# A recurrence with packed side work: one piece per step from the group's start, bare steps last, and gelus in halves

## The chip, the core and the metric
The kernel is one program on one core of a Trainium2 chip. The metric is the device time of one execution in microseconds (us), of which the median of three runs is shown. Five engines run side by side, each in its own order: TensorE (PE, with its weight loads as PEld), VectorE (DVE), ScalarE (ACT), GpSimd (POOL) and SyncE (SP). They meet only at semaphores.

## What is computed
The input x has 4 sequences of 1024 tokens with 128 features. The reference is a chain of six layers:

```python
x = x + 0.5 * _L0_ffn_ref(_layernorm(x), ...)      # small attention over 4 positions, then 8 experts, top 2
x = x + _L0_attn_ref(_layernorm(x), ...)           # hierarchical attention
x = x + 0.5 * _L0_ffn_ref(_layernorm(x), ...)      # the same expert layer again
x = x + 0.5 * _L1_ffn_ref(_layernorm(x), ...)      # sign weights, 128 -> 512 -> 128
x = x + _L1_attn_ref(_layernorm(x), ...)           # recurrence of 1024 steps, then an MLP 128 -> 512 -> 128
x = x + 0.5 * _L1_ffn_ref(_layernorm(x), ...)      # sign weights again
```

The recurrence inside `_L1_attn_ref` is the part that can't be spread out:

```python
def step(state, inp):                               # state is 4 x 32
    xb_t, xd_t = inp
    state = jnp.tanh(state @ A.T + xb_t)
    out = state @ C.T + xd_t
    return (state, out)
```

## The kernel before
The program has three phases: the first expert layer, the hierarchical attention, and `routed_ffn_and_recurrence`, which merges the last four layers. The change touches only the third phase.

**Groups and steps.** The 1024 tokens are cut into 8 groups (`GROUPS`) of 128 tokens. Once two groups have been prepared, the third phase enters a loop over groups 0 to 7, and `body(g)` runs the 128 recurrence steps of group g on two engines. On PE, a step waits for the last tanh and issues one product of 4 columns (L1369). On ACT, a step waits for that product and takes one tanh (L1514). PE and ACT hand the state to each other 1024 times, so this is a chain that nothing shortens.

**Pieces.** All other work of the last four layers is cut into pieces that PE issues behind a step's product, before the next step's. `slots(g)` gives each piece the number of the step (its slot) in which it stands. These are the kinds, by the names that the prediction uses:
- a *small piece*: `up_half` or `k_up_half`, 256 columns against one weight tile (L1170, L1231), or `down_tile` of an expert, two products of 128 columns (L1180)
- a *transpose piece*: four 128x128 transposes (L1105), as `p_turn1`, `p_turn2`, `p_turn3` and `k_turn_tiles`
- a *large piece*: `k_down_tile` (L1242), four products of 128 columns; `p_proj` (L1132) has as many
- a *whole run*: several `up_whole` or `k_up_whole` of 512 columns (L1157, L1223) in one slot
- a *mix piece*: half of `mix_tiles` (L1264, L1266), which reads the recurrence's states with a stride as weights; two per group
- `p_qkv` (384 columns, L1119), `p_router` (L1145) and `input_product` (L1253), the last of which starts the next group's sums
- a *bare step* has no piece at all.

**What a group holds.** In group g the *expert part* (`routed_order`) computes the expert layer of group g+2: a whole run of four with the first expert's down tiles, then for each of the other experts 4 up halves and 4 down tiles, with the attention pieces of groups g+3 and g+4 between them. The *dense part* (`dense_order`) holds three 128 -> 512 -> 128 layers of three groups: a (sign weights, group g+1), r (the MLP, group g-1) and z (the last sign weights, group g-2). The mix pieces hand the recurrence's output of group g-1 to DVE, which makes r's input of it. Groups 6 and 7 have no expert part left.

**What sets the order.** `slots` gives each piece an assumed cost from the table `NS` and spreads the pieces over all 128 steps in proportion to it, so bare steps lie between pieces everywhere. ACT's gelus are put into slots by `plan_of`, one step or two behind their up piece. DVE's order is written out in `routed(m, g)` and `dense(g)`: norms, expert sums (`add_expert`, L882), layer outputs and the attention's elementwise work. POOL computes reciprocal roots. After the loop PE does the mix of group 7, then z of group 6, r of group 7 and z of group 7, one after another (L1400 on).

## Time and profile before
| | us |
|---|---|
| median of 3 runs (2312.71 to 2322.3) | 2315.91 |
| the profiled execution | 2301.93 |
| its span | 2300.1 |
| first tanh of the loop to the last | 1137.31 to 2249.13 |
| PE busy (matmul) | 1856.1, 81% |
| ACT busy | 830.5, 36% |
| DVE busy | 1010.4, 44% |
| mean granted TensorE clock | 0.745 |

The page gives the busy time of each engine over the whole span. Matmuls are pipelined, so a busy PE is not one at its peak. Its second part cuts the span in 40 slices and has a row PEclk with the clock that TensorE was granted, in tenths of full speed. The loop of 1024 steps takes the second half of the span. The timeline view has the single instructions, and behind each the idle time of its engine before it and what ended that.

### The profile page before, as it was taken

How to read it: one execution, taken by the hardware profiler on the slowest of the kernel's cores; microseconds unless marked ns; L12 is line 12 of the kernel's file. 1: busy time of each engine (PE TensorE's matmuls, PEld its weight loads, DVE VectorE, ACT ScalarE, POOL GpSimd, SP SyncE). 2: the span in 40 equal slices, each digit the busy share in tenths (PEclk: the TensorE clock that was granted, in tenths of full speed). 3: DMA queues.
4: the chain of work that ended last, by engine and by line, in shares of the span. 5: the costliest groups of instructions: out<-in, count | busy, mean ns of one | idle time of the engine just before them, and what ended most of it. 6: DMA issues, size and time to landing. Idle time of an engine off the chain costs nothing.

```text
span 2300.1 us, 36406 instructions
## 1 busy us (share of the span) xinstructions
PE 1856.1 (81%) x13438; PEld 1328.0 (58%) x13438; DVE 1010.4 (44%) x3005; ACT 830.5 (36%) x2192; POOL 193.5 (8%) x314
## 2 busy tenths in 40 slices
PE   2889995848688596758788998999989999978776
PEld 1666674536474474726655655666666666645555
DVE  3666654866777767645522223223232221121102
ACT  1444443546556464413333223233242222322222
POOL 1212201000010000021101001010000000000000
PEclk8999996979789697859986558577595555765557
DMA  5000000000000000000000000000000000000000
GB/s 151 1 1 1 0 1 1 2 1 3 2 2 2 1 2 2 2 0 1 1 1 1 1 0 1 0 1 5 1 5 1 1 5 0 1 5 1 5 0 14
DMA packets 12015, 13.06 MB, mean 6 GB/s; under 512 B 1649, under 2 KB 10641, under 8 KB 11281
## 3 DMA queue, kind: packets, MB, share of 16 engines
q1 hardware_dynamic: 11840, 10.77, 1.8%
q8 instruction: 105, 1.72, 0.3%
q14 instruction: 70, 0.57, 0.1%
HBM read 8.67 MB, written 2.10 MB: 5 GB/s over the span
## 4 chain that ended last, share of the span: by engine, by line
issue 53%; POOL 3%; POOLq 2%; PE 0%; DVE 0%; ACT 0%; ACTq 0%; SPq 0%; DVEq 0%
POOL m_pairs L706 1%; POOLq L673 1%; POOL m_root_p L716 0%; POOL m_roots L697 0%; POOL m_root_r L716 0%; POOLq L715 0%; POOL m_root_a L716 0%; POOL m_root_z L716 0%; PE m_post_misc L1242 0%; PE m_down L1231 0%; PE m_up L1231 0%; POOLq L688 0%; POOL m_roots L690 0%; POOLq L686 0%; POOLq L684 0%
## 5 line engine op out<-in xcount | busy, mean ns | idle before, releaser
L1514 ACT ACTIVATE m_state<-m_scan 32x4 f32<-32x4 f32 x1024 | 166.3, 162 | 776.8 <-PE m_scan L1369 776.0
L1369 PEld LDWEIGHTS m_scan<-m_state,rnnA 128*32 128x32 f32 x2048 | 173.4, 131 | 375.3 <-issue 191.8
L1369 PE MATMUL m_scan<-m_state,rnnA 128*32 128x4 f32 x2048 | 262.0, 198 | 107.4 <-ACT m_state L1514 107.4
L882 DVE SCALAR_TENSOR_TENSOR x_all<-m_down,m_weight,x_all 128x128 f32<-128x128 f32 x256 | 71.9, 343 | 447.6 <-PE m_down L1180 447.6
L1180 PE MATMUL m_down<-moe,m_hT 128*128 128x128 f32 x1024 | 242.2, 390 | 4.8 <-ACT m_hT L1460 3.7
L1180 PEld LDWEIGHTS m_down<-moe,m_hT 128*128 128x128 f32 x1024 | 193.9, 272 | 14.0 <-ACT m_hT L1460 5.7
L1170 PE MATMUL m_up<-m_x2T,moe 128*128 128x256 f32 x384 | 189.8, 606 | 5.0 <-ACT m_hT L1460 5.0
L2157 DVE TENSOR_TENSOR att_big<-at_ring,att_big 128x512 f16<-128x512 f32 x192 | 123.9, 685 | 49.0 <-ACT att_big L1839 48.2
L286 PEld LDWEIGHTS f_down<-moe,f_hT 128*128 128x128 f32 x1024 | 125.6, 195 | 27.9 <-issue 26.5
L1839 ACT ACTIVATE att_big<-at_ring 128x512 f16<-128x512 f32 x192 | 111.4, 596 | 66.1 <-PE at_ring L1972 64.0
L277 PE MATMUL f_up<-f_x2T,moe 128*128 128x512 f32 x256 | 123.6, 608 | 5.8 <-ACT f_hT L193 5.8
L286 PE MATMUL f_down<-moe,f_hT 128*128 128x128 f32 x1024 | 127.3, 278 | 0.0
L463 DVE SCALAR_TENSOR_TENSOR x_all<-f_down,f_weight,x_all 128x128 f32 (+1 forms) x256 | 72.0, 344 | 82.8 <-PE f_down L286 82.7
L1972 PE MATMUL at_ring<-at_keys,att_Mhi 128*128 128x512 f16 x256 | 81.6, 402 | 30.8 <-DVE at_coarse_q L2144 18.9
L193 ACT ACTIVATE f_hT<-f_up 128x512 f32<-128x512 f32 x128 | 74.9, 597 | 69.4 <-PE f_up L277 68.6
L2264 DVE SCALAR_TENSOR_TENSOR att_big<-at_ring,att_big 128x512 f16<-128x512 f32 x128 | 80.8, 682 | 27.1 <-ACT att_big L1880 27.0
L1170 PEld LDWEIGHTS m_up<-m_x2T,moe 128*128 128x128 f32 x384 | 86.0, 271 | 11.0 <-ACT m_hT L1460 6.7
L2062 PE MATMUL at_s<-att_Nhi,att_big 128*128 128x128 f16 x1024 | 92.3, 221 | 0.0
L1880 ACT ACTIVATE att_big<-at_ring 128x512 f16<-128x512 f32 x128 | 68.7, 602 | 61.6 <-PE at_ring L2053 61.2
L2062 PE MATMUL at_s<-att_Nlo,att_big 128*128 128x128 f16 x512 | 88.9, 221 | 0.0
L1991 PE MATMUL at_s<-at_keys,att_big 128*128 128x16 f16 x768 | 72.1, 172 | 18.4 <-DVE att_big L2157 18.4
L1991 PEld LDWEIGHTS at_s<-at_keys,att_big 128*128 128x128 f16 x768 | 64.5, 99 | 38.2 <-issue 19.4
(330 smaller groups left out, 3217.5 us busy)
## 6 DMA issues: line engine op xcount, KB each, us to landing
x_all<-in_x SPq DMA_DIRECT2D x4, 512.0 KB, 6.0
...
```

Of the source, the lines that this page charges most:

```text
L277: nc.tensor.matmul(up[c % UP_RING][:, :], w1[:, c * 128:(c + 1) * 128], x2T[b][:, :], start=True, stop=True).then_inc(s_up, 1)
L286: last = nc.tensor.matmul(down[e % 2][:, s * 128:(s + 1) * 128], hT[c % H_RING][:, s * 128:(s + 1) * 128], w2[:, c * 128:(c + 1) * 128], s ...
L1170: ins = nc.tensor.matmul(up[c % 2][:, part], w1[:, c * 128:(c + 1) * 128], x2T[m % 2][:, part], start=True, stop=True)
L1180: ins = nc.tensor.matmul(down[:, s * 128:(s + 1) * 128], hT[c % H_RING][:, s * 128:(s + 1) * 128], w2[:, c * 128:(c + 1) * 128], start=(c ...
L1369: nc.tensor.matmul(scan[b][0:STATE, NB * t:NB * (t + 1)], rnnA[:, :], last, start=False, stop=(t == 127), skip_group_check=True).then_inc( ...
L1514: nc.scalar.activation(state[b][0:STATE, NB * t:NB * (t + 1)], scan[b][0:STATE, NB * t:NB * (t + 1)], ACT.Tanh).then_inc(s_tanh, 1)
L1839: nc.scalar.activation(XH[c % 2][:, :, h, :], ring[n % RING][:, :].rearrange("p (q i) -> p q i", i=BLK), ACT.Copy).then_inc(s_xhi, 1)
L1972: last = nc.tensor.matmul(ring[n % RING][:, :], att[w][:, h * D:(h + 1) * D], src(lo), start=(i == 0), stop=(i == 2))
L1991: nc.tensor.matmul(o, lh, keys[:, blk, 0, :], start=True, stop=False)
L2062: last = nc.tensor.matmul(sbk[t % 2][:, 0:D], y[t % 2][:, h, :], att[w][:, h * D:(h + 1) * D], start=(h == 0 and n == 0), stop=(h == HEADS ...
L2157: dve.tensor_tensor(XL[c % 2][:, :, h, :], ring[n % RING][:, :].rearrange("p (q i) -> p q i", i=BLK), XH[c % 2][:, :, h, :], ALU.subtract) ...
L2264: dve.scalar_tensor_tensor(YL[t % 2][where], ring[n % RING][:, :].rearrange("p (h t) -> p h t", h=HH), Y_UP / (X_UP * A_UP), YH[t % 2][whe ...
```

## The change
It alters `routed_ffn_and_recurrence` alone, in five ways.
1. `slots` no longer spreads by cost. It gives each piece the next slot, from 0 on, and `(pause, (n,))` in an order skips n slots. What steps are left stand bare at the group's end.
2. The orders of the pieces move. The mix pieces stand behind the first up halves and not ahead of them. The attention pieces stand one expert later, and the four `p_qkv` stand between down tiles. The router stands in the dense part. A whole run of the dense part has four `k_up_whole` where it had three and two halves.
3. Groups 6 and 7 have orders of their own (`last_orders`), and z of group 6 moves from behind the loop into group 7. PSUM banks and waits follow.
4. ACT takes each expert chunk's gelu as two instructions of 256 columns, except for the four chunks of the whole run. Its copies for the attention pieces stand in the slot of their piece.
5. DVE's order follows: `v_logits`, `v_scores` and `v_shift` go behind the expert part or into `dense`, and the last two groups have functions of their own.

```diff
             def between(e, m, f, j, g):
 
                 out_ = []
-                if e == 2 and real(j):
+                if e == 3 and real(j):
                     out_ += [(p_turn2, (j,))]
...
-                if e == 7 and real(j):
+                if e == 7 and real(j) and g < 0:
                     out_ += [(p_router, (j,))]
...
-                if real(g - 1):
-                    order += [(mix_tiles, (g - 1, i)) for i in range(2)]
                 for e in range(EXPERTS):
                     if e:
                         order += ups(e + 1)
+                    if e == 1 and real(g - 1):
+                        order += [(mix_tiles, (g - 1, i)) for i in range(2)]
                     if real(m) and e:
-                        order += [(down_tile, (m, e, s)) for s in range(NB)]
+                        for s in range(NB):
+                            order += [(down_tile, (m, e, s))]
+                            if e == 6 and g >= 0 and real(m + 2):
+                                order += [(p_qkv, (m + 2, s))]
...
+            def last_orders(g):
+
+                r, z = ("r", g - 1), ("z", g - 2)
+                if g == GROUPS - 2:
+                    a = ("a", g + 1)
+                    order = [(k_turn_tiles, a)] + k_run(*a, None, range(FC)) + [(k_turn_tiles, z)]
+                    order += [(mix_tiles, (g - 1, i)) for i in range(2)] + k_downs(*a, range(NB)) + [(pause, (3,)), (k_turn_tiles, r), (pause, (2,))]
+                    order += k_ups(*r, a, range(FC)) + k_ups(*z, r, (0,)) + k_downs(*r, (0, 1)) + [(k_turn_tiles, ("p", g + 1))]
+                    order += k_ups(*z, r, (1,)) + k_downs(*r, (2, 3)) + k_ups(*z, r, (2, 3))
+                    return order + [(pause, (2,))] + k_downs(*z, range(NB)) + [(input_product, (g + 1,))]
+                late = ("z", g - 1)
+                order = [(k_turn_tiles, z)] + k_run(*z, None, range(FC)) + [(mix_tiles, (g - 1, i)) for i in range(2)]
+                order += k_downs(*z, range(NB)) + [(pause, (3,)), (k_turn_tiles, r), (pause, (2,))] + k_ups(*r, z, range(FC))
+                order += [(pause, (2,))] + k_downs(*r, range(NB))
+                return order + [(pause, (12,)), (k_turn_tiles, late), (pause, (2,))] + k_ups(*late, r, range(FC)) + [(pause, (2,))] + k_downs(*late, range(NB))
...
             def slots(g):
 
-                order = routed_order(g + 2, g) + dense_order(g)
-                tied = lambda n: n > 0 and (order[n][0] in (up_whole, k_up_whole) and order[n - 1][0] is order[n][0]
-                                            or order[n][0] is down_tile and order[n][1][1] == 0)
-                total = sum(NS[f] for n, (f, _) in enumerate(order) if not tied(n))
-                at, slot, out_ = 0, 0, []
+                order = routed_order(g + 2, g) + dense_order(g) if real(g + 2) else last_orders(g)
+                runs = (up_whole, k_up_whole)
+                slot, out_ = 0, []
                 for n, (f, args) in enumerate(order):
-                    if not tied(n):
-                        slot = int(128 * (at + NS[f] / 2) / total) if n else 0
-                        at += NS[f]
+                    tied = n > 0 and (f in runs and order[n - 1][0] is f or n < 8 and f is down_tile)
+                    if f is pause:
+                        slot += args[0]
+                    elif n and not tied:
+                        slot += 1
                     out_.append((slot, f, args))
+                assert slot < 127
                 return out_
...
-                def gelu(m, c):
-
-                    act.wait_ge(s_up, ONE + CHUNKS * m + c + 1)
-                    act.wait_ge(s_down, ONE + EXPERTS * m + (max(c - H_RING, -2)) // 2 + 1)
-                    nc.scalar.activation(hT[c % H_RING][:, :], up[c % 2][:, :], ACT.Gelu_apprx_tanh).then_inc(s_h, 1)
+                def gelu(m, c, cols=((0, 512),)):
+
+                    for at, end in cols:
+                        if at == 0:
+                            act.wait_ge(s_up, ONE + CHUNKS * m + c + 1)
+                            act.wait_ge(s_down, ONE + EXPERTS * m + (max(c - H_RING, -2)) // 2 + 1)
+                        ins = nc.scalar.activation(hT[c % H_RING][:, at:end], up[c % 2][:, at:end], ACT.Gelu_apprx_tanh)
+                        if end == 512:
+                            ins.then_inc(s_h, 1)
```

The dense part's new order in groups 0 to 5 is: the whole run of a, the router, 4 small pieces of r, 4 large of a, 4 small of r, then z's first small pieces and r's large ones in turn, the transposes for the next mix and z's last small pieces, a pause of two steps, z's 4 large pieces, a pause of two and the input product. Group 0, which has no r and z yet, has a pause of nine after a's large pieces.

**Place 1: PE, start of group 3.** Each `m_scan` row is the product of one step, or of two where x2 stands; `m_post_misc` with `rnnC` and `rnnD` is mix.

Before:

```order
L1369 MATMUL m_scan1<-m_state1,rnnA 32x4 x2
L1105 MATMUL m_post_misc<-ident,m_xn_z 128x128 x4
L1369 MATMUL m_scan1<-m_state1,rnnA 32x4 x2
L1264 MATMUL m_post_misc<-rnnC,m_state0 128x128
L1266 MATMUL m_post_misc<-rnnD,m_nT_p0 128x128
L1264 MATMUL m_post_misc<-rnnC,m_state0 128x128
L1266 MATMUL m_post_misc<-rnnD,m_nT_p0 128x128
L1369 MATMUL m_scan1<-m_state1,rnnA 32x4 x2
```

After:

```order
L1147 MATMUL m_post_misc<-ident,m_xn_z 128x128 x4
L1445 MATMUL m_scan1<-m_state1,rnnA 32x4
L1212 MATMUL m_up0<-m_x2T1,moe1 128x256
L1445 MATMUL m_scan1<-m_state1,rnnA 32x4
L1212 MATMUL m_up0<-m_x2T1,moe1 128x256
L1445 MATMUL m_scan1<-m_state1,rnnA 32x4
L1212 MATMUL m_up1<-m_x2T1,moe1 128x256
L1445 MATMUL m_scan1<-m_state1,rnnA 32x4
L1212 MATMUL m_up1<-m_x2T1,moe1 128x256
L1445 MATMUL m_scan1<-m_state1,rnnA 32x4
L1308 MATMUL m_post_misc<-rnnC,m_state0 128x128
L1310 MATMUL m_post_misc<-rnnD,m_nT_p0 128x128
```

Four small pieces have moved ahead of the mix, and the steps around it are no longer bare.

**Place 2: PE, group 0, the two transpose pieces in the middle of the expert part.** `m_turn<-ident,m_xn1` is `p_turn1`, `m_pre_misc<-ident,m_xn_a` turns a's input.

Before:

```order
L1180 MATMUL m_down<-moe2,m_hT1 128x128
L1369 MATMUL m_scan0<-m_state0,rnnA 32x4 x2
L1105 MATMUL m_turn<-ident,m_xn1 128x128 x4
L1369 MATMUL m_scan0<-m_state0,rnnA 32x4 x3
L1105 MATMUL m_pre_misc<-ident,m_xn_a 128x128 x4
L1369 MATMUL m_scan0<-m_state0,rnnA 32x4 x2
L1170 MATMUL m_up0<-m_x2T0,moe1 128x256
```

After:

```order
L1222 MATMUL m_down<-moe2,m_hT3 128x128
L1445 MATMUL m_scan0<-m_state0,rnnA 32x4
L1147 MATMUL m_turn<-ident,m_xn1 128x128 x4
L1445 MATMUL m_scan0<-m_state0,rnnA 32x4
L1147 MATMUL m_pre_misc<-ident,m_xn_a 128x128 x4
L1445 MATMUL m_scan0<-m_state0,rnnA 32x4
L1212 MATMUL m_up0<-m_x2T0,moe1 128x256
```

The two pieces stood among four bare steps and now stand in adjacent slots, with small pieces right before and behind.

**Place 3: PE, behind the loop.** The last mix product, then what follows it.

Before:

```order
L1264 MATMUL m_post_misc<-rnnC,m_state1 128x128
L1266 MATMUL m_post_misc<-rnnD,m_nT_p1 128x128
L1105 MATMUL m_pre_misc<-ident,m_xn_z 128x128 x4
L1231 MATMUL m_down<-m_nT_z,bin1 128x256 x2
L1231 MATMUL m_up0<-m_nT_z,bin1 128x256 x2
```

After:

```order
L1308 MATMUL m_post_misc<-rnnC,m_state1 128x128
L1310 MATMUL m_post_misc<-rnnD,m_nT_p1 128x128
L1147 MATMUL m_post_misc<-ident,m_xn_r 128x128 x4
L1274 MATMUL m_up0<-m_nT_r,mlp1 128x256 x2
L1274 MATMUL m_up1<-m_nT_r,mlp1 128x256 x2
```

The layer z of group 6 is gone from here, and r of group 7 follows the mix at once.

## Rows read from the trace of the kernel before

**Rows 1.** The page: the group of the 1024 tanhs.

```profile
L1514 ACT ACTIVATE m_state<-m_scan 32x4 f32<-32x4 f32 x1024 | 166.3, 162 | 776.8 <-PE m_scan L1369 776.0
```

**Rows 2.** Windows view, groups 0 to 7, then the part behind the loop.

```profile
1137.30:1259.20 121.90, 99.76 (x532) 66.55 (x533) 35.88 (x145) 38.95 (x166) 11.29 (x19) 0.76 0.00 1
1259.20:1409.60 150.40, 137.22 (x603) 90.73 (x602) 42.54 (x163) 42.22 (x173) 12.47 (x21) 0.62 0.00 1
1409.60:1565.20 155.60, 145.75 (x657) 96.72 (x655) 44.44 (x166) 45.75 (x183) 12.40 (x21) 0.65 0.00 1
1565.20:1719.40 154.20, 143.18 (x656) 96.26 (x654) 44.44 (x166) 45.56 (x182) 12.40 (x21) 0.67 0.01 2
1719.40:1884.60 165.20, 154.51 (x642) 106.36 (x641) 38.70 (x144) 43.11 (x175) 6.03 (x10) 0.56 0.01 2
1884.60:2027.40 142.80, 131.12 (x618) 88.04 (x616) 29.37 (x111) 40.38 (x171) 4.82 (x8) 0.67 0.01 3
2027.40:2146.90 119.50, 92.19 (x434) 62.96 (x434) 16.97 (x51) 29.66 (x153) 3.61 (x6) 0.52 0.01 3
2146.90:2249.30 102.40, 74.95 (x374) 51.02 (x374) 11.17 (x34) 26.53 (x144) 2.41 (x4) 0.50 0.01 3
2249.30:2300.10 50.80, 35.02 (x172) 28.72 (x172) 13.12 (x37) 10.05 (x24) 2.41 (x4) 0.80 0.05 16
```

The columns are: stretch in us from the span's start, its length, then for PE, PEld, DVE, ACT and POOL the busy us with the number of instructions, the granted clock, the DMA share and GB/s.

**Rows 3.** Timeline of ACT: tanhs at full clock, with the idle time before each.

```profile
1572.45 0.16 ACT L1514 ACTIVATE m_state<-m_scan 32x4 f32<-32x4 f32 x1 [0.58 <-PE m_scan L1369]
...
1575.96 0.16 ACT L1514 ACTIVATE m_state<-m_scan 32x4 f32<-32x4 f32 x1 [2.87 <-PE m_scan L1369]
...
1681.89 0.16 ACT L1514 ACTIVATE m_state<-m_scan 32x4 f32<-32x4 f32 x1 [0.62 <-PE m_scan L1369]
...
1688.47 0.16 ACT L1514 ACTIVATE m_state<-m_scan 32x4 f32<-32x4 f32 x1 [0.32 <-PE m_scan L1369]
1689.71 0.16 ACT L1514 ACTIVATE m_state<-m_scan 32x4 f32<-32x4 f32 x1 [1.08 <-PE m_scan L1369]
```

**Rows 4.** Timeline of ACT: tanhs at half clock.

```profile
1579.73 0.16 ACT L1514 ACTIVATE m_state<-m_scan 32x4 f32<-32x4 f32 x1 [3.09 <-PE m_scan L1369]
...
1618.99 0.16 ACT L1514 ACTIVATE m_state<-m_scan 32x4 f32<-32x4 f32 x1 [1.08 <-PE m_scan L1369]
...
2075.82 0.16 ACT L1514 ACTIVATE m_state<-m_scan 32x4 f32<-32x4 f32 x1 [2.04 <-PE m_scan L1369]
...
2206.25 0.16 ACT L1514 ACTIVATE m_state<-m_scan 32x4 f32<-32x4 f32 x1 [1.19 <-PE m_scan L1369]
2206.77 0.16 ACT L1514 ACTIVATE m_state<-m_scan 32x4 f32<-32x4 f32 x1 [0.36 <-PE m_scan L1369]
```

**Rows 5.** Windows view, stretches of groups 0, 3 and 4 by clock.

```profile
1142.30:1186.70 44.40, 38.10 (x264) 26.45 (x262) 18.88 (x71) 15.58 (x74) 5.32 (x10) 1.00 0.00 1
1186.70:1231.60 44.90, 40.10 (x167) 26.48 (x166) 4.41 (x16) 10.58 (x51) 3.31 (x4) 0.50 0.00 1
1572.90:1575.90 3.00, 2.81 (x10) 2.30 (x10) 1.71 (x7) 0.16 (x1) 0.66 (x2) 0.98 0.00 0
1575.90:1674.50 98.60, 94.40 (x364) 63.19 (x363) 23.29 (x79) 21.59 (x95) 5.72 (x8) 0.50 0.00 1
1674.50:1679.90 5.40, 4.75 (x8) 1.84 (x8) 3.87 (x15) 3.88 (x9) 0.94 (x2) 0.66 0.00 2
1824.96:1835.20 10.24, 8.68 (x57) 5.75 (x57) 0.00 (x0) 4.97 (x21) 0.00 (x0) 1.00 0.01 2
1835.20:1884.60 49.40, 45.87 (x194) 33.07 (x194) 9.07 (x30) 11.78 (x52) 2.41 (x4) 0.50 0.00 0
```

**Rows 6.** Timeline of PE in group 0, the second transpose piece, before the clock's fall.

```profile
1184.16 0.66 PE L1105 MATMUL m_pre_misc<-ident,m_xn_a 128*128 128x128 f32 x4
```

**Rows 7.** Timeline behind the loop: r's norm is done, and its transposes.

```profile
2260.89 1.12 DVE L905 TENSOR_SCALAR m_xn_r<-m_mixed,m_mv_r,m_root_r 128x128 f32<-128x128 f32 x4 [1.46 <-POOL m_root_r L716]
...
2267.85 0.47 PEld L1105 LDWEIGHTS m_post_misc<-ident,m_xn_r 128*128 128x128 f32 x4
```

229 lines of the change are left out of this document (132 added, 97 removed).

## The prediction

> **What bounds the kernel now.** I read the page first. The 1024 tanhs of the recurrence take 166.3 us of ACT, and ACT sits idle 776.8 us before them, nearly all of it for PE's product of the step [rows 1]. So the loop lasts as long as PE takes to come round to the next product. What counts is the length of a step, which is the idle time before a tanh plus the tanh's own 0.16.
>
> I then read the loop group by group in the windows view [rows 2]. The eight groups take 121.9, 150.4, 155.6, 154.2, 165.2, 142.8, 119.5 and 102.4 us, and 50.8 us follow behind them. The granted clock differs: 0.76 in group 0, near 0.5 in groups 6 and 7. DVE is busy at most 44.4 us of a group and POOL 12.5, so neither bounds it.
>
> Third, the timeline gives the price of one step of each kind at both levels of the clock, 2.4 GHz [rows 3] and 1.2 GHz [rows 4]:
> - bare: 0.32 + 0.16 = 0.48 at full clock, 0.52 at half
> - small piece: 0.78 and 1.35, so half clock costs 0.57
> - transpose piece: 0.74 and 1.24, costs 0.50
> - large piece: 1.24 and 2.20, costs 0.96
> - mix piece: 3.03 and 3.25, nearly the same, as its weight loads bind.
>
> A bare step hardly feels the clock, and every piece does. So I asked where the clock falls and rises [rows 5]. In group 3 it fell at the first mix piece and stayed at half for 98.6 us, although PE was busy 94.40 of them. It rose in the whole run of the dense part (1674.50 to 1679.90) and held behind it. In group 4 it fell again at 1835.2, where bare steps lay between large pieces, and the last 49.4 us ran at half. In group 0 it fell at 1186.7, behind two transpose pieces among bare steps [rows 5, 6].
>
> **The change, part by part.** Negative is saved time.
>
> *Group 0: -18 us.* It has no mix. Packed, no bare step parts its pieces before the whole run, so I take full clock until its first pause. In the 44.9 us at half clock before [rows 5] stand 18 small pieces, 4 `p_qkv`, one transpose piece and the router: 18 x 0.57 = 10.3, plus 0.5. `p_qkv` and the router never ran in the loop at full clock. For `p_qkv` the bounds are a small piece's 0.78 and a large piece's 1.24 plus ACT's copy of 0.5, and I take 1.3 against about 1.9 before: -2.3 for four. The router lies between the transpose and the large piece; 1.2 against 2.0 is -0.8. The whole run of four at full clock against three and two halves: -2. The wait in front of the last transpose piece shrinks behind the pause of nine (-3.5). Against this stand 0.9 for gelus that a's first large piece, now two slots behind the run, waits for, 1 for copies in their piece's slot, and 47 bare steps at half clock, +1.5. The sum is -15.5. Adding slots one by one over the new group gives 101.6 us, or -20. I take -18.
>
> *Groups 1, 2, 3: -5, -4, -4.* The mix stays, two pieces of 3.0 and 3.25 us back to back. I expect the clock to fall there again, and the expert part behind it to stay at half, since up to eight adjacent pieces did not raise it [rows 5]. Won are the four small pieces now ahead of the mix (4 x 0.57 = 2.3), the router behind the run (0.8), tighter `p_qkv` (1 to 1.5). Some 22 bare steps at the end cost 0.04 each, 0.9. Group 1 also loses two late waits, about 1.
>
> *Group 4: -19.* Its dense part held 12 small and 9 large pieces at half clock [rows 5]: 6.8 + 8.7, plus 1.4 for a transpose piece and the input product. I expect no fall there, as the bare steps between are gone: -16.9. The rest is 2.3 + 0.8 - 0.9.
>
> *Group 5: -1.5* (2.3 less 0.9).
>
> *Group 6: -7.* Pieces by count: 4 transpose 4.5, a whole run 6.1, mix 6.3, 16 small at half clock 21.6, 12 large, input product 1.3, waits for DVE's copies 1.8, 92 bare 47.8. Eight of the large pieces stand in fours without a gap. Four adjacent at half clock never occurred before, so a four costs between 8.8 (all half) and 5.0 (all full). I take 7.3, because the whole run, the nearest thing without bare steps, did raise the clock. With 14.6 and 8.8 the sum is 112.8 against 119.5.
>
> *Group 7: +7.* It takes over z of group 6: 3 transpose 3.7, run 6.1, mix 6.3, 16 small 21.6, three fours of large pieces 21.9, a wait 0.9, 94 bare 48.9; 109.4 against 102.4.
>
> *Behind the loop: -6.5.* r's norm began at 2260.89 and was done about 2262.0, but PE reached its transposes only at 2267.85 [rows 7], because z of group 6 stood ahead. Its 5.9 us go, and DVE's copy for z (0.7) too, though the 8 up halves then start cold; -6.5 is near the upper end, 3 the lower.
>
> *Gelus in halves: 0.* Two halves cost ACT 0.46 each where one whole took 0.60, but a step with a small piece at full clock leaves ACT 0.62 idle [rows 3]. *DVE and POOL: 0.* Their work is the same, and the cover is a step chain that leaves DVE idle for two thirds of a group. Pieces that wait for DVE are again at least four slots behind their source, except those counted.
>
> *Before the loop: 0.* The two halves of the order there gain and lose a wait of about 1.5 us each.
>
> Sum: -18 - 13 - 19 - 1.5 - 7 + 7 - 6.5 = **-58**. The profiled execution took 2301.93 with a span of 2300.1, which gives a span of 2242. Its time stands 14 below the median of 2315.91. I carry the difference to the median: **2258 us**. An effect below 0.5%, 12 us, can't be told from none.
>
> **The rivals.**
>
> *The transposes let the clock fall in group 0.* It fell right behind the second one [rows 6]. If it does again, the last 12 small pieces of the expert part run at half: 6.8, plus 1.9, 0.5 and 2.6 for `p_qkv`, transposes and run; 12 us, so 2270. Against it, bare steps stood around them then. Chance 0.14. The Trainium skill (TensorE: Matmul & The Clock Gate, Part 4) says that transposes do not count as PE-busy; by that rule it would fall, and the trace allows that.
>
> *The packed half-clock stretch raises the clock itself.* Then groups 1 to 5 win the 48 small pieces behind the mix, 27.4 each, and some 4.2 each for transposes, `p_proj` and `p_qkv`: 158 us, so 2100. The row that speaks against it has PE busy 94.40 of 98.60 us at half clock [rows 5]. The same page of the Trainium skill ("Why this matters for your kernels") says that continuous busy time brings the full clock; this trace disagrees, if busy is what the profile counts. Chance 0.06.
>
> *Slower: the dense parts fall to half clock.* Behind the whole run now stands the router, eight tiny products, and then r's pieces. Should the clock fall there in each group as it did in group 4, the dense part costs 16 x 0.57 + 12 x 0.96 + 1.4 = 22.1 in groups 2 to 5, 13.7 in group 1, 5 in group 0: 107 us more than forecast, 2365. It is slower than before once four of the six fall. For it: one of five fell before [rows 5]. Against: that one had bare steps between large pieces. Chance 0.04. With two or three falling the time is within 0.5%: 0.05.
>
> *The split does not hide.* If both halves add their excess, 2 x 0.46 - 0.60 = 0.32, to 12 chunks of six groups, 23 us: 2281. Chance 0.05.
>
> **How the numbers follow.** The forecast has 0.66, with its own range of 2240 to 2278 from the fours (+8 to -11) and the other bounds (about 8). The range of 2225 to 2285 adds the first and last rival and one falling dense part, and lets the 0.06 and the 0.09 go. Faster is 0.66 + 0.14 + 0.06 + 0.05 = 0.91, the same 0.05, slower 0.04.
>
> **What the profile would show.** Right: group 0 near 104 us with full clock until its run; groups 1 to 3 at half clock from mix to run and full behind it; group 4 near 146; group 7 longer than before; r's transposes within a microsecond of its norm. Wrong: an expert part at full clock behind the mix, half clock behind a whole run, or ACT as what PE waits for in small-piece steps.

## The result, and the profile after

The changed kernel takes **2221.22 us** (runs of 2216.25 to 2240.87), the kernel before, run beside it, 2319.11: a ratio of 0.959 with a 95% interval of 0.952 to 0.966. Forecast were 2258 and a range of 2225 to 2285. The direction was right; the gain was 98 us where 58 were forecast, and the time lies below the range. The profiled execution took 2225.43 us (span 2223.6). Of all runs named below, one of the second thin mix (2240.5) and one with the order before the loop put back (2247.51) were slow by over 1.5%, and without them those two medians would be 0.03 and 5.1 us lower.

The page's line of the tanhs, which answers to [rows 1]:

```profile
L1582 ACT ACTIVATE m_state<-m_scan 32x4 f32<-32x4 f32 x1024 | 166.1, 162 | 695.3 <-PE m_scan L1445 694.7
```

PE is still what the recurrence waits for, 81.5 us less. The windows view by group, then behind the loop, answers to [rows 2] and has its columns:

```profile
1128.00:1236.80 108.80, 87.85 (x530) 61.19 (x531) 35.98 (x145) 40.25 (x177) 11.31 (x19) 0.80 0.00 1
1236.80:1384.20 147.40, 134.40 (x601) 89.84 (x600) 42.62 (x163) 43.04 (x185) 12.42 (x21) 0.62 0.00 1
1384.20:1522.80 138.60, 130.10 (x653) 89.73 (x652) 44.62 (x166) 45.93 (x194) 12.43 (x21) 0.73 0.01 3
1522.80:1672.60 149.80, 142.09 (x653) 95.32 (x652) 44.62 (x166) 45.81 (x193) 12.42 (x21) 0.66 0.01 2
1672.60:1817.40 144.80, 134.56 (x641) 92.18 (x640) 38.93 (x144) 43.39 (x188) 6.03 (x10) 0.67 0.01 3
1817.40:1961.20 143.80, 130.23 (x617) 88.27 (x616) 30.18 (x112) 40.85 (x183) 4.83 (x8) 0.67 0.01 3
1961.20:2066.30 105.10, 80.53 (x433) 55.41 (x434) 16.53 (x49) 29.56 (x152) 3.87 (x6) 0.63 0.01 3
2066.30:2177.60 111.30, 85.93 (x418) 57.80 (x418) 13.16 (x36) 29.78 (x152) 2.42 (x4) 0.58 0.02 5
2177.60:2223.60 46.00, 28.71 (x120) 22.57 (x120) 11.08 (x33) 6.72 (x16) 2.41 (x4) 0.72 0.02 6
```

Against [rows 2], with the forecast in brackets: group 0 -13.1 (-18), group 1 -3.0 (-5), **group 2 -17.0 (-4)**, group 3 -4.4 (-4), group 4 -20.4 (-19), group 5 +1.0 (-1.5), **group 6 -14.4 (-7)**, group 7 +8.9 (+7), behind the loop -4.8 (-6.5), and **before the loop -9.3 (0)**. The sum is -76.5, against the -58 forecast.

Single stretches in the same view, which answer to [rows 5]: group 0 at full clock, group 1 from mix to the end of its expert part, and group 2 on both sides of 1442:

```profile
1134.80:1192.80 58.00, 55.44 (x343) 37.31 (x341) 24.79 (x96) 25.04 (x105) 8.90 (x15) 1.00 0.00 1
1250.90:1336.20 85.30, 85.30 (x316) 56.87 (x317) 24.46 (x86) 19.85 (x88) 6.00 (x10) 0.50 0.00 1
1397.60:1442.00 44.40, 44.40 (x170) 31.03 (x170) 12.74 (x48) 9.07 (x45) 1.21 (x2) 0.50 0.00 1
1442.00:1472.70 30.70, 29.90 (x176) 19.22 (x175) 14.59 (x49) 14.65 (x57) 5.73 (x8) 1.00 0.00 1
```

The busy share of PE does not tell the levels apart: it is 95.6% at 2.4 GHz in group 0 (55.44 of 58.00) and 100% at 1.2 GHz in group 1. In group 2 the clock rose inside a packed expert part, as the timeline of ACT shows in the length of the steps, 1.35, then 2.20 (`p_proj`), then 0.74 and 0.78:

```profile
1439.94 0.16 ACT L1582 ACTIVATE m_state<-m_scan 32x4 f32<-32x4 f32 x1 [1.19 <-PE m_scan L1445]
1442.15 0.16 ACT L1582 ACTIVATE m_state<-m_scan 32x4 f32<-32x4 f32 x1 [2.04 <-PE m_scan L1445]
1442.90 0.16 ACT L1582 ACTIVATE m_state<-m_scan 32x4 f32<-32x4 f32 x1 [0.58 <-PE m_scan L1445]
1443.68 0.16 ACT L1582 ACTIVATE m_state<-m_scan 32x4 f32<-32x4 f32 x1 [0.62 <-PE m_scan L1445]
```

Group 2 shows one more thing. Behind the whole run of its dense part, which took 4.3 us at full clock, and the router, the clock fell again for 10.2 us, and one small piece and a's four large ones ran at half:

```profile
1472.70:1482.90 10.20, 10.20 (x46) 8.43 (x44) 1.04 (x4) 2.15 (x9) 0.00 (x0) 0.50 0.00 0
```

Full clock in group 0 ended at 1192.8, behind the whole run, while a's first large piece waited for gelus (timeline of PE):

```profile
1193.53 2.08 PE L1285 MATMUL m_pre_misc<-bin,m_h_a 128*128 128x128 f32 x8 [1.73 <-ACT m_h_a L1533]
```

### The profile page after: what moved, and what is told of

The parts are those of the page before. It is cut to its first block, busy times and chain, and to the rows that moved or that the text cites. A ratio compares the mean times of both kernels' runs of the same rounds, so it can differ in the third digit from the quotient of the medians.

```text
span 2223.6 us, 36427 instructions
## 1 busy us (share of the span) xinstructions
PE 1791.9 (81%) x13416; PEld 1288.1 (58%) x13416; DVE 1011.1 (45%) x3005; ACT 835.0 (38%) x2264; POOL 194.0 (9%) x314
## 4 chain that ended last, share of the span: by engine, by line
issue 51%; POOL 3%; POOLq 2%; PE 0%; DVE 0%; ACT 0%; ACTq 0%; SPq 0%; DVEq 0%
POOL m_pairs L707 1%; POOLq L674 1%; POOL m_root_p L717 0%; POOL m_roots L698 0%; POOL m_root_r L717 0%; POOLq L716 0%; POOL m_root_a L717 0%; POOL m_root_z L717 0%; PE m_post_misc L1285 0%; PE m_up L1274 0%; POOLq L689 0%; POOLq L687 0%; POOL m_roots L691 0%; POOLq L685 0%; POOLq L682 0%
## 5 line engine op out<-in xcount | busy, mean ns | idle before, releaser
L1222 PE MATMUL m_down<-moe,m_hT 128*128 128x128 f32 x1024 | 229.1, 374 | 3.1 <-DVE x_all L889 3.1
L1222 PEld LDWEIGHTS m_down<-moe,m_hT 128*128 128x128 f32 x1024 | 183.7, 259 | 13.3 <-issue 7.4
L1212 PE MATMUL m_up<-m_x2T,moe 128*128 128x256 f32 x384 | 171.5, 554 | 1.6 <-ACT m_hT L1524 1.5
L2040 PE MATMUL at_ring<-at_keys,att_Mhi 128*128 128x512 f16 x256 | 81.6, 402 | 31.6 <-DVE at_coarse_q L2212 18.7
L1524 ACT ACTIVATE m_hT<-m_up 128x256 f32<-128x256 f32 (+1 forms) x200 | 86.2, 433 | 27.5 <-PE m_up L1212 20.3
```

The lines of the kernel that those rows point to most:

```text
L1212: ins = nc.tensor.matmul(up[c % 2][:, part], w1[:, c * 128:(c + 1) * 128], x2T[m % 2][:, part], start=True, stop=True)
L1222: ins = nc.tensor.matmul(down[:, s * 128:(s + 1) * 128], hT[c % H_RING][:, s * 128:(s + 1) * 128], w2[:, c * 128:(c + 1) * 128], start=(c ...
L1524: ins = nc.scalar.activation(hT[c % H_RING][:, at:end], up[c % 2][:, at:end], ACT.Gelu_apprx_tanh)
L2040: last = nc.tensor.matmul(ring[n % RING][:, :], att[w][:, h * D:(h + 1) * D], src(lo), start=(i == 0), stop=(i == 2))
```

## The experiments

Each kernel starts from the changed one unless the text says "before". Times are medians of runs beside runs of the kernel before (2320.4 to 2323.0). The table has the length of each group in us, from the windows view of the profiled execution. Each row is one execution.

| kernel | time | 0 | 1 | 2 | 3 | 4 | 5 | 6 | 7 |
|---|---|---|---|---|---|---|---|---|---|
| before, second | 2323.95 | 140.6 | 157.4 | 154.4 | 153.9 | 146.8 | 159.5 | 118.3 | 102.4 |
| before, third | 2318.97 | 140.7 | 149.2 | 155.2 | 154.1 | 146.9 | 159.2 | 119.8 | 102.5 |
| changed, again | 2216.09 | 108.8 | 147.4 | 138.6 | 138.8 | 146.7 | 144.8 | 104.7 | 111.4 |
| before, packed | 2255.38 | 111.9 | 153.6 | 150.8 | 156.9 | 148.9 | 146.6 | 100.0 | 96.6 |
| spread evenly | 2231.84 | 111.0 | 148.5 | 151.1 | 132.6 | 147.0 | 142.2 | 112.3 | 113.3 |
| spread by cost | 2303.78 | 132.8 | 148.7 | 151.5 | 153.8 | 151.0 | 157.0 | 117.1 | 115.8 |
| mix ahead | 2092.83 | 108.9 | 117.9 | 121.7 | 120.4 | 122.5 | 123.5 | 99.9 | 101.9 |
| before, mix ahead | 2161.67 | 128.8 | 128.0 | 132.1 | 120.2 | 133.4 | 118.7 | 119.9 | 102.4 |
| last version | 2063.54 | 109.2 | 114.3 | 120.6 | 118.4 | 116.1 | 114.9 | 92.8 | 98.4 |

### Both kernels again: how much of a group is its execution

No edit.

> The changed kernel once more, unedited, beside the edits of it that follow. Its runs so far lay between 2216.25 and 2240.87 us, its profiled execution at 2225.43, that of the kernel before 14 below its median. Theory A: my miss is partly that I carried those 14 us over as if they belonged to both kernels; which execution is profiled is chance, so the profiled time of this run stands within some 10 us of its own median on either side, and the groups whose clock rose in the middle (group 2 at about 1442 us, group 6) may rise elsewhere or not at all. Theory B: the places at which the clock rises are fixed by the order of the pieces, so every group comes back within 2 us. By A group 2 can cost up to 12 us more than its 138.6; by B it is 138.6 again.

Measured: 2216.09 (2215.91 to 2216.46). Seven groups agree within 1.9 us; group 3 took 138.8 in place of 149.8, at a mean clock of 0.73 in place of 0.66, because the clock now rose in its middle as it had in group 2:

```profile
1523.60:1662.40 138.80, 130.47 (x653) 88.73 (x652) 44.62 (x166) 45.85 (x194) 12.44 (x21) 0.73 0.01 3
```

Here it rose 72.8 us into the group, behind two adjacent transpose pieces, where in group 2 it had risen 57.8 us in, at `p_proj` (timeline of PE):

```profile
1595.32 1.12 PE L1147 MATMUL m_pre_misc<-ident,m_xn_a 128*128 128x128 f32 x4
1596.36 0.23 PE L1445 MATMUL m_scan<-m_state,rnnA 128*32 128x4 f32 x2
1596.52 0.70 PE L1212 MATMUL m_up<-m_x2T,moe 128*128 128x256 f32 x2
```

So theory A holds for group 3 and theory B for group 2. The kernel before, twice:

> The kernel before, unedited, to see a second execution's trace. Its runs lie between 2299.57 and 2334 us, the profiled one at 2301.93. Theory: the difference is the clock, which changes level at other places from one execution to the next; then any execution near 2315 or more shows one or two groups 8 to 18 us longer at a lower mean clock, and the rest within 0.3 us of the first. Rival: it is the stretch in front of the loop (loads), and the groups agree within 1 us.

> The same once more, for a third execution of the kernel before. By the theory another group may differ than in the second; by the rival the eight groups last 121.9, 150.4, 155.6, 154.2, 165.2, 142.8, 119.5 and 102.4 again within 1 us.

Measured: 2323.95 and 2318.97. The first three rows are the second execution's groups 0, 4 and 5, the last two its group 0 in parts:

```profile
1136.20:1276.80 140.60, 118.65 (x532) 79.69 (x533) 36.00 (x145) 38.95 (x166) 11.23 (x19) 0.59 0.00 1
...
1742.50:1889.30 146.80, 136.12 (x643) 93.41 (x642) 38.71 (x144) 42.96 (x175) 6.03 (x10) 0.67 0.01 3
1889.30:2048.80 159.50, 146.52 (x616) 98.82 (x614) 29.40 (x112) 40.53 (x171) 4.83 (x8) 0.57 0.01 2
...
1145.30:1164.80 19.50, 16.65 (x112) 11.25 (x112) 9.60 (x35) 6.96 (x35) 2.54 (x6) 1.00 0.01 1
1164.80:1250.40 85.60, 76.77 (x306) 49.67 (x306) 15.50 (x57) 22.48 (x99) 5.72 (x8) 0.50 0.00 0
```

Against [rows 2] group 0 is 18.7 us longer, group 1 7.0 longer, group 4 18.4 shorter, group 5 16.7 longer. In group 0 the clock fell at 1164.8, three steps behind `p_turn2`, where bare steps alternate with single pieces; in the execution I had read it stayed full through the same steps up to 1186.7 [rows 5]. The loops lasted 1133.3 and 1127.6 us against 1112.0, and the spans are 22.1 and 17.1 us longer than mine. So what sets the executions apart is nearly all the clock in the loop's groups, and with it the 14 us between my profiled execution and the median; my prices for groups 0, 4 and 5 belonged to one execution.

### The gelus in halves

In the kernel before, the halves alone; in the changed one, whole gelus again:

```diff
- p.append((until(until(at + 1, down_tile, m, c // 2), up_half, m, c + 2), gelu, (m, c)))
+ p += [(until(until(at + 1 + half, down_tile, m, c // 2), up_half, m, c + 2), gelu,
+        (m, c, ((256 * half, 256 * half + 256),))) for half in range(2)]
```

> The kernel before with one part of the change alone: each gelu outside the dense runs as two instructions of 256 columns. Theory (the prediction's term of 0): the halves hide behind the pieces, time within 0.3% of before (2308 to 2322 us). Rival 1 (does not hide): the excess of 0.32 us for 12 chunks of six groups, +23 us. Rival 2 (the halves are the gain): in the kernel before bare steps lie between the pieces, and a whole gelu of 0.60 us in front of a tanh makes a bare step of 0.48 longer, to 0.76, where a half makes it 0.62; if a third of the 96 expert gelus meet such a step, that is 32 x 0.28 less what the second half costs in its own step, 32 x 0.14, so 4 to 5 us gained.

> The changed kernel with every gelu whole again (0.60 us in one step in place of 0.46 in each of two). Theory: packed pieces leave ACT idle in every step, so this is within 0.4% of the changed kernel, and group 0, which runs at full clock, lengthens by at most 2 us. Rival (the halves matter at full clock, where a small piece is 0.78 us long and a tanh plus a whole gelu are 0.16 + 0.60): each whole gelu at full clock holds the next tanh by 0.1 to 0.3 us, 12 of them in group 0 and some 8 in group 2, so 2 to 6 us more than the changed kernel, seen as idle time of ACT's tanh that is ended by ACT itself, and group 0 at 111 to 113 us against 108.8.

Measured: 2313.89 for the halves in the kernel before, ratio 0.996 (0.990 to 1.001), every group within 0.2 us of [rows 2]; 2226.28 for whole gelus, every group within 0.2 us of the changed kernel's first profiled execution. Group 0 took 108.8 with both. The prediction's 0 holds, and both rivals fall. The changed kernel beside it had 2216.09, and their runs do not overlap (2224.32 and more against 2216.46 and less). The groups show where these 10 us lie: group 3 took 150.0 with whole gelus and 138.8 in that execution, by its clock. Whether the halves have a part in that rise is not shown; the changed kernel's first execution had 149.8 with them.

### Where the mix stands, and what it does to the clock

The mix in four quarters with three small pieces between each, then with four and DVE's sums of experts 1 and 2 ahead of its use of the mix:

```diff
- if e == 1 and real(g - 1):
-     order += [(mix_tiles, (g - 1, i)) for i in range(2)]
+ for i in range(NB):
+     order.insert(at + (MIX_GAP + 1) * (i + 1) - 1, (mix_tiles, (g - 1, i)))
```

> The changed kernel with the mix (two pieces of 3.0 us) as four quarters, three small pieces between each; the same work. Theory: it is the stretch of 6 us of the mix, in which TensorE mostly loads small strided weights and few columns flow, that brings the clock to its lower level, and without that the expert parts of groups 1 to 5 run at full clock as group 0's does: 16 small pieces less 4 that were ahead of the mix, 48 in all of 5 groups, 0.57 each, plus some 4 for transposes, p_proj and p_qkv in each group, less what group 2 has already (its clock rose at 1442): about 31 x 4 + 17 = 140 us less, so near 2080. Rival 1: anything below a dense run's flow lets the clock fall, the mix is just the first such place; then the clock falls a few pieces later and the time is within 1% of the changed kernel. Rival 2: four quarters load the same weights and a single quarter is enough to let the clock fall: same time as the changed kernel, plus 1 us a group for more slots with a piece in them.

> The thin mix (four quarters) once more, four small pieces between two quarters, and DVE's sums of experts 1 and 2 ahead of its copy of the mix, so that the down tiles no longer wait for that copy (4.47 us of step 17 of group 1 and 4.52 of step 18 of group 2 in the run before). Theory A: with the first thin mix, group 2 passed all four quarters at full clock and fell only in the step with that wait; without the wait the expert parts of groups 1 to 5 stay at full clock, near 2090. Theory B: the quarters leave so little streaming that it falls by chance in some groups; each group that falls costs 26 to 31 us, so 2120 to 2200. Theory C: the wait was not the reason, and it falls again in every group at about step 15: 2215.

Measured: 2221.32 and 2206.96. The first is within 1% of the changed kernel, as both its rivals had it, and not near 2080. In it group 1 took 130.3 and group 2 147.1; the first down tile of expert 2 waited for DVE's sum, which stood behind the mix's copy (timeline of PE, group 1):

```profile
1263.03 1.19 PE L1222 MATMUL m_down<-moe,m_hT 128*128 128x128 f32 x4 [3.08 <-DVE x_all L889]
```

In the second that wait is gone and the clock fell all the same, seven to twelve steps behind the whole run of groups 1 to 5. That is nearest to theory C: the wait was not the reason, and theory A's 2090 was wrong. Thinning the mix is not enough.

The mix with adjacent weights (its products are other ones than the reference's):

```diff
- state[g % 2][0:STATE, :].rearrange("p (t s) -> p s t", s=NB)[:, s, :],
+ state[g % 2][0:STATE, s * 128:(s + 1) * 128],
```

> The changed kernel with the mix's weights read from adjacent columns in place of every fourth one (the mix then multiplies other columns than the reference asks for). Theory A: what makes a mix piece 2.8 to 3.25 us long at either clock is the load of strided weights; adjacent ones cost it 1.2 to 1.5 at full clock as a large piece, 3.3 us less for each of 8 mixes, 26 in all, and as TensorE is no longer starved there, the clock keeps its level: another 26 to 31 in groups 1, 3, 4, 5 and 17 in group 2, some 130; near 2070. Theory B: strided reading costs nothing, fp32 weights load slowly anyway: 2216. Between: the piece shortens but the clock falls all the same, 2190.

Measured: 2114.19. A mix piece's step fell from 2.80 to 1.82 us at full clock, from one step's product to the next (timelines of PE, first the changed kernel, then this one):

```profile
1247.45 0.23 PE L1445 MATMUL m_scan<-m_state,rnnA 128*32 128x4 f32 x2
...
1250.25 0.23 PE L1445 MATMUL m_scan<-m_state,rnnA 128*32 128x4 f32 x2
```

```profile
1390.48 0.23 PE L1445 MATMUL m_scan<-m_state,rnnA 128*32 128x4 f32 x2
...
1392.30 0.22 PE L1445 MATMUL m_scan<-m_state,rnnA 128*32 128x4 f32 x2
```

Groups 2 and 3 kept full clock from run to end and took 112.4 and 112.5; the others fell as before (145.7, 142.5, 140.7):

```profile
1235.00:1380.70 145.70, 132.71 (x601) 87.96 (x600) 42.65 (x163) 43.07 (x186) 12.43 (x21) 0.62 0.00 1
1380.70:1493.10 112.40, 103.73 (x653) 71.00 (x652) 44.64 (x166) 45.77 (x193) 12.44 (x21) 0.94 0.01 3
```

So with adjacent weights the clock can pass the mix, which it did in groups 1 to 5 of no profiled execution of the changed kernel, but in groups 1, 4 and 5 it fell at the second mix piece all the same. The edit makes the piece shorter and its loads quicker at once, so which of the two helps is not shown. Where the clock held, the group took 112.4 us against 138.6 for group 2 and 149.8 or 138.8 for group 3 of the changed kernel.

The mix ahead of the run, with z's transposes, and DVE's copies to match:

```diff
  order = []
+ if real(g - 2) and g - 2 != GROUPS - 2:
+     order += [(k_turn_tiles, ("z", g - 2))]
+ if real(g - 1):
+     order += [(mix_tiles, (g - 1, i)) for i in range(2)]
  if real(m):
      order += [(up_whole, (m, c, g)) for c in range(4)]
```

> The changed kernel with z's transpose piece and the two mix pieces ahead of the whole run of each group, in place of five small pieces behind it (DVE's copies of z and of the mix ahead of expert 0 to match). The same work, the same number of pieces. Theory A: a whole run brings full clock, and what ended it in groups 1 to 5 was the stretch of 6 us in which the mix loads strided weights; with the mix in front, where the clock is at half anyway, the run raises it and packed small pieces keep it, as group 0 shows for 60 steps. Then the expert parts of groups 1 to 5 run at full clock: 26 to 31 us in each but group 2, which has 11 of them already, about 125 us in all, so near 2090. The first such run showed that spreading the mix alone moves group 1 by 17 us and the other groups by little, with a new wait of 4.5 us in each. Theory B: packed small pieces cannot hold full clock for a whole expert part, group 0 is the exception since nothing of a dense part waits in it; then the clock falls some 20 steps in and the time is 2170 to 2216. Theory C: the move costs a wait (the mix now waits for DVE's copy of z, expert 0's for the mix): 1 to 2 us a group, 5 to 10 more than the changed kernel if nothing else changes, 2226.

Measured: **2092.83**, ratio 0.903 (0.895 to 0.910), 2090 expected. Groups 1 to 5 took 118 to 124 us; group 3 from its run to the bare steps:

```profile
1498.40:1589.40 91.00, 86.76 (x560) 60.27 (x560) 36.67 (x123) 37.76 (x163) 8.14 (x12) 1.00 0.01 4
```

Theory A holds: the same pieces keep 2.4 GHz for 91 us once the mix no longer stands behind the run. The edit moves z's transposes too, but they are not what ended full clock: group 1 has no z and fell at the mix as well, and with adjacent weights groups 2 and 3 kept full clock with z's transposes behind the run. In groups 4 and 5 the clock still fell once, late in the expert part. Theory C holds in part as well, since the mix now waits 3.6 us for DVE's copy of z:

```profile
1484.73 0.80 PE L1308 MATMUL m_post_misc<-rnnC,m_state 32*128 32x128 f32 x2 [3.58 <-DVE m_nT_z L930]
```

The same move in the kernel before, bare steps spread:

> The kernel before, bare steps spread by its planner, with z's transposes and the mix ahead of the whole run of each group. Theory A (packing and the mix's place work together): with bare steps between the pieces full clock doesn't outlast the first third of an expert part, so each of groups 1 to 5 gains 5 to 12 us and the waits for DVE's copy of z cost 1 to 3: 2270 to 2300. Theory B (the mix alone keeps the clock down): groups 1 to 5 gain 26 to 31 us each, as in the changed kernel, and the time is near 2190.

Measured: **2161.67**, ratio 0.931 (0.925 to 0.937). That is theory B and beyond, as its time was 2190: 22 to 34 us in each of groups 1 to 5 against [rows 2], 13 to 41 against the second execution. With bare steps between the pieces full clock lasted 41.0 us in group 1 and 92.1 in group 3, so theory A's "doesn't outlast the first third" was wrong. One short edit gives more than the whole change; the change then adds 69 us to it.

`p_proj` twice in a row:

```diff
- out_ += [(p_proj, (j,))]
+ out_ += ([(p_proj_early, (j,))] if g >= 0 else []) + [(p_proj, (j,))]
```

> The changed kernel with p_proj issued twice in a row in groups 0 to 5, so two large pieces stand adjacent behind the down tiles of expert 4 (the same products into the same bank, so extra work of 1.24 us at full clock or 2.2 at half in each group). Theory A: large pieces among small ones are what raises the clock in the middle of a half-clock expert part, as at step 37 of group 2, and two of them do it in every group; then the clock rises at steps 37 to 39 of groups 1 to 5 and about 25 small pieces and four p_qkv behind it run at full clock: some 15 us less in groups 1, 3, 4 and 5 (group 2 had it), less 6 x 1.5 for the extra pieces: near 2170. Theory B: the rise at step 37 is chance that an extra piece doesn't favour: 2216 to 2240.

Measured: 2226.01, and the clock rose at `p_proj` in group 2 alone, as theory B had it. Set side by side, the profiled executions say more than "chance". In all five whose pieces stand as in the changed kernel (the two of it, whole gelus, this one with its extra piece, and the order before the loop put back) group 2 rose at `p_proj`, 58 to 59 us in. Group 3, with the same pieces in the same order, rose in one of the five, and group 1 in another one. So the order of the pieces alone does not decide it, and what does stays open.

### Packing, and where bare steps stand

The changed orders over the 126 steps, evenly, and then by the cost table of the kernel before (here the pauses are left out, and the table alone places the bare steps); and the kernel before with one piece a step:

```diff
+ out_ = [(at * 126 // top, f, args) for at, f, args in out_]          # evenly
- slot = int(128 * (at + NS[f] / 2) / total) if n else 0               # before, packed
+ slot += 1
```

> The changed kernel's orders, banks and halves, but with the pieces of each group spread evenly over its 126 steps, bare steps between them, as the kernel before had them. Theory: the packing is most of the change. Then group 0 is back near 120 (from 108.8), group 4 near 160 (from 144.8) and group 6 near 115, with groups 1, 3 and 5 within 3 us; sum +45 to +75, so 2265 to 2290. Rival: the new orders and banks carry the gain, packing only moves bare steps: within 0.5% of the changed kernel.

> The changed kernel's orders with the bare steps between the pieces where the planner of the kernel before puts them (by its cost of each piece, so that more bare steps stand around large pieces, transposes and the mix). The even spread of the run before took 111.0 us for group 0 and 147.0 for group 4, near the packed 108.8 and 144.8, against 121.9 and 165.2 before the change. Theory A: what let the clock fall in groups 0 and 4 before the change is bare steps around the large pieces, which my terms for packing (-18, -19) rest on; then group 0 returns to 118 to 122 and group 4 to 160 to 165, and the time to 2265 or more. Theory B: the new order of the pieces did it (p_qkv between down tiles, router behind the run, a run of four); then group 0 stays near 111, group 4 near 147, the time within 1% of the even spread's 2232.

> The kernel before with packing alone: its own orders, whole gelus, one piece a step from step 0 on and all bare steps last. No pauses stand in it, so transposes and pieces that follow their source wait for ACT and DVE. Theory A (packing carries the gain by the clock): group 0 falls from 121.9 by 10 or more although about 5 us of new waits appear in it, group 4 from 165.2 to 150 or less, the time 2240 to 2280. Theory B (the order carries it): group 0 keeps a stretch at half clock in its expert part, group 4 one in its dense part, and the new waits of 2 to 5 us a group make it slower than before, 2320 to 2350.

Measured: 2231.84, 2303.78 and 2255.38. The same pieces in the same order differ by 72 us with where the bare steps stand. Group 0 has 21.8 of them, group 3 21.2 (in the even spread its clock rose inside the expert part, right behind `p_proj` and r's transposes) and group 5 14.8. Group 0 by each (windows; first the even spread at full clock, then the spread by cost up to and behind its fall):

```profile
1134.30:1193.60 59.30, 49.67 (x333) 33.53 (x333) 18.32 (x68) 23.09 (x114) 4.37 (x9) 1.00 0.00 1
```

```profile
1134.80:1163.80 29.00, 24.37 (x165) 16.56 (x166) 11.75 (x45) 11.57 (x59) 3.16 (x7) 1.00 0.00 1
1163.80:1234.60 70.80, 62.04 (x248) 39.59 (x248) 11.12 (x43) 18.51 (x85) 5.73 (x8) 0.52 0.00 1
```

By cost, `p_turn2` and the pieces next to it have a bare step on both sides, and the clock falls there, at 1164.5, as in the kernel before's second execution at 1164.8. Evenly, no more than two bare steps stand among five, and it holds. Theory A holds for the spread by cost in the time and in group 0, whose 132.8 is more than it said; group 4, for which it said 160 to 165, stayed at 151.0. My expectation for the even spread, 2265 to 2290, was wrong. The time of the old order packed is what its theory A had (2240 to 2280). It gains 67 us of the 98, the new order with the old spacing 19 (ratio 0.993, 0.989 to 0.997). Of the 67, groups 6 and 7 give 18 to 20 and 6 us in each comparison with the three executions of the kernel before, so that part does not hang on which one is taken.

### Before the loop

PE's, ACT's and DVE's orders in front of the loop as they were:

```diff
+ if g < 0:
+     if e == 2 and real(j): out_ += [(p_turn2, (j,))]
...
+     return out_
```

> The changed kernel with the order of the routed pieces in front of the loop put back to what it was before (attention's pieces one expert earlier on PE, ACT and DVE). Theory: the 9.3 us that the stretch in front of the loop became shorter, for which I had forecast 0, come from these places alone: PE there waited 1.2 to 1.8 us each for ACT's and DVE's copies around turn2, turn1, p_qkv and turn3. Then group 0 starts 7 to 10 us later than in the changed kernel (1135 to 1138 in place of 1128 to 1129), and the loop lasts as long as before within what its clock varies by itself. Rival: the shortening is from something else of the change, and it starts at 1128 to 1131.

Measured: 2219.39 with group 1 at 129.9 by its clock. From the first transposes of this part to the first step, in the windows view, changed and put back:

```profile
980.00:1128.00 148.00, 108.14 (x566) 80.48 (x566) 77.17 (x300) 46.85 (x79) 29.05 (x47) 0.83 0.00 1
```

```profile
978.40:1134.70 156.30, 110.69 (x566) 82.49 (x566) 77.35 (x300) 45.53 (x79) 29.00 (x47) 0.83 0.00 1
```

It is 156.3 in the kernel before too, and 148.0 again in the changed kernel's second execution. The theory holds: 8.3 us from placing attention's pieces one expert later.

### A version that beats both

On top of the mix ahead: DVE picks the weights behind the copy of z; the mix ahead of the run in groups 6 and 7; `p_qkv` in two experts; group 0's pauses split.

```diff
+ if own and g >= 1: v_weights(m)                       # was at the end of dense()
+ order = [(k_turn_tiles, z), (k_turn_tiles, a)] + mix + k_run(*a, None, range(FC))
```

> The kernel with the mix ahead of the whole run (2092.83), with what its trace shows to be left: DVE picks the experts' weights (3.4 us of small operations, L857 to L881) behind its copy of z's transposes and not ahead of it, which holds the first mix piece for 3.6 us in groups 2 to 5 (-14); the mix stands ahead of the run in groups 6 and 7 too and r's transposes right behind it, without the pauses for its norm (-9 to -12 each, if the pieces behind the run keep full clock); p_qkv in two experts' down tiles, every second tile, in place of one's four, since the clock fell there in groups 4 and 5 (-5 each); four of group 0's nine pause steps ahead of a's large pieces, which wait 4 us for gelus (-2). Theory A (the clock follows how much of its time TensorE streams): all of it works, 2093 - 14 - 21 - 10 - 2 = 2046. Theory B (the pieces' order fixes it only by chance): the waits go (-16), and each group may gain or lose up to 8 by the clock, so 2065 to 2090.

Measured: 2074.52. The wait of 3.6 is gone, but the split pauses cost 2.2 in group 0, group 7 took 104.1, and groups 4 and 5 fell with no `p_qkv` in them: that placing could not have helped there. The time is in theory B's range, 2065 to 2090, and far from theory A's 2046.

```diff
- v_resid(g - 1)            # ahead of add_expert(m, 6)
+ v_resid(g - 1)            # behind it; p_qkv and pauses back; 4 small pieces of r before a's large ones
```

> The version with the mix ahead of the run and the experts' weights behind the copy of z (2074.52), changed where its trace shows losses: DVE adds r's residual (three operations of 0.69 us) behind the sum of expert 6, not ahead of it, since the first down tile of expert 7 waited 1.2 to 1.6 us for that sum in groups 4 and 5 and the clock fell there; p_qkv back among one expert's tiles; group 0's pauses back behind a's large pieces (the split of them let the clock fall and cost 2.2); in groups 6 and 7 four small pieces of r stand between the run and the large pieces that wait for its gelus (waits of 1.8 and 2.8 us). Theory A (the wait for DVE ends full clock in groups 4 and 5): no fall ahead of the run in them, 5 to 6 us less each, 2 in group 0, 3 to 5 in groups 6 and 7 each: near 2055. Theory B (the small pieces of experts 6 and 7 themselves don't hold it): groups 4 and 5 lose the wait of 1.2 us alone, 2063 to 2068.

Measured: 2064.37, in theory B's range. Group 7 took 99.6; groups 4 and 5 still waited 1.2 us each for that sum (1.16 and 1.15 idle) and fell, so the two theories were not told apart.

```diff
- if e == 5 and g >= 0 and real(g + 1):      # a's transposes; DVE's sum of expert 6 ahead of their copy
+ if e == 6 and g >= 0 and real(g + 1):      # and turn3 behind expert 6
```

> The best version so far (2064.37) with a's transposes and turn3 between the last down tile of expert 6 and the first of expert 7, where no up halves stand, so that DVE's sum of expert 6 is done before that tile wants the bank (it waited 1.16 us in group 4 and 1.73 in group 5, and the clock fell in that step or the next). Theory A (the wait ends full clock): full clock holds from the run to the bare steps in groups 4 and 5, 1.2 + 2.6 us less in group 4 and 1.7 + 4.0 in group 5, and about 1 less of waits in groups 0 to 3: 2052 to 2056. Theory B: the clock falls there all the same, 2060 to 2063.

Measured: **2063.54** (2062.43 to 2064.28), ratio 0.890 (0.884 to 0.896). Full clock held in groups 4 and 5 from the run to the bare steps:

```profile
1609.70:1695.00 85.30, 81.31 (x532) 57.56 (x532) 32.02 (x109) 34.34 (x149) 4.83 (x8) 1.00 0.01 4
1726.00:1811.40 85.40, 78.63 (x510) 54.93 (x510) 24.86 (x83) 33.28 (x148) 3.62 (x6) 1.00 0.02 4
```

That much is as theory A had it: with the wait gone the clock held. They gave 2.4 and 5.0 us where theory A had 3.8 and 5.7, with waits of 1.2 and 1.7 in them; the waits that went were 1.16 and 1.15. The edit moved two transpose pieces along with the wait, so the wait as the sole cause is likely, not shown. The time did not follow: it is just above theory B's 2060 to 2063, not 2052 to 2056. The whole run of the dense part took 5.29 in place of some 5.05 us in groups 1 to 3 and 5.04 in place of 4.30 in group 0, and group 2 lost 1.8 in all. The eight groups together took 4.9 us less (884.7 against 889.6), but the version before it was profiled in the slowest of its four runs (2068.95), and the medians differ by 0.8 alone.

This version is 158 us faster than the changed kernel and 257 faster than the one before. One loss in it remains: from the first transposes to the first step it takes 151.3 us where the changed kernel takes 148.0, and the version with the mix ahead has the same 151.3. DVE's changed order stands in that part too; no run tests whether it is the reason.

## Why the prediction was right, and where it failed

The time fell 4 us below the range. The forecast span was 2242; it became 2223.6. That is half of the miss of 37; the other half is the step from the profiled execution to the median. In the span, group 2 (-13.0), the part before the loop (-9.3) and group 6 (-7.4) gave more than forecast, group 0 gave less (+4.9), and the six other terms differ by 2.5 or less.

- **"I carry the difference to the median."** This step cost 18 us: the 14 carried, and 4 that the changed kernel's median lies below its profiled execution. The second and third execution show what the 14 were, groups at half clock. They said nothing about another kernel. This is the step that put the time outside the range: without the 14 the forecast is 2244 and the range 2211 to 2271. The forecast would still have been 23 above the measured time.
- **Group 0, -18.** Measured -13.1. Full clock held up to the run, through both adjacent transpose pieces, as forecast. The loss was sized wrongly: I had 0.9 for the wait for gelus; that step took 4.0 us where a large piece takes 1.24, and the clock fell in it, so that the next two large pieces took 2.21 and 2.09. Against the other two executions the same term is -32. (The term's parts add up to -16.0, not to the -15.5 written; -18 stood on the slot-by-slot sum as well.)
- **Groups 1 to 3, -5, -4, -4.** Right in the mechanism (the mix ends full clock) and near in size in groups 1 and 3 (-3.0 and -4.4). In group 2 "I expect the expert part behind it to stay at half, since up to eight adjacent pieces did not raise it" failed: it rose at `p_proj`, and the group gained 13 us more than forecast. It did so in every profiled execution with these pieces, five of five, while groups 3 and 1 rose in one each. Group 2 showed both signs that the prediction had called wrong, an expert part at full clock behind the mix and half clock behind a whole run (1472.7 to 1482.9).
- **Group 4, -19.** Measured -20.4, but for this execution only; the two others of the kernel before had 146.8 and 146.9 in group 4, and 159.5 and 159.2 in group 5. In the changed kernel's first execution the dense parts of groups 4 and 5 held full clock up to their bare steps, as forecast. It is luck that the execution I read had its fall in the group that I priced. And packing does not rule out a fall in a dense part, as group 2 shows.
- **Group 6, -7.** Measured -14.4, and not by the term that I had in doubt. The two fours took 8.7 and 6.6 us, 15.3 together where I had 14.6 (7.3 each, range 5.0 to 8.8). What I had at half clock without asking is the rest: the clock rose at r's first pair of large pieces (2.21, then 1.85 us), and the transposes, six small pieces and the second pair behind it ran at full clock. That is 3.4 us on the 16 small pieces (18.2 for 21.6), 2.3 on r's four large ones (6.55 for 8.8) and 1.0 on the transposes; the mean clock was 0.63 in place of 0.52.
- **Groups 5 and 7, behind the loop.** +1.0, +8.9 and -4.8 against -1.5, +7 and -6.5.
- **Before the loop, 0.** "The two halves of the order there gain and lose a wait of about 1.5 us each" was wrong: it gained 8.3 us, confirmed by putting the order back, and 1.0 of the -9.3 lies before that part. I had put the term at nothing without a row.
- **Gelu halves, 0.** Right, as far as the groups show. An expert's half takes ACT 0.37 us, less than the 0.46 that I had for it. **DVE and POOL, 0.** Nothing in the groups speaks against it, though no run tests it by itself.
- **The forecast's own range.** 2240 to 2278 is a slip at its upper end: +8 and about 8 give 2274. The outcome does not hang on it.

Of the rivals, the slower ones did not occur, except for the one short fall in group 2's dense part. *The transposes let the clock fall in group 0*: not when packed. Among bare steps they may have a part in it: in all three executions of the kernel before, group 0 fell within a few steps behind a transpose piece. No run takes the transposes away and leaves the bare steps, so this is not shown, and in the even spread the clock passed the same pieces with fewer bare steps beside them. The Trainium skill (TensorE: Matmul & The Clock Gate, Part 4) says that a transpose "doesn't count as PE-busy the same way"; this trace does not bear it out as a rule for the fall, with two adjacent ones inside 58.00 us at 1.00, and in group 3 of the second execution the clock rose at 1596.36, right behind two adjacent ones. That they weigh less is not refuted. *The packed half-clock stretch raises the clock itself* (0.06, 2100) came true in one group of five and failed in the others. The forecast treated it as all or nothing, where the groups differ, and so the range did not reach down to one group's 13 us.

What I did not see is that the mix's place is worth more than the change. The prediction had both halves of it, that the mix ends full clock and that a run brings it, and did not ask what follows when they change places: 128 us in the changed kernel (2221.22 to 2092.83), 159 in the one before (2320.42 to 2161.67).
